# Tails of attentions 3 and 4: batch 2's sum, root and shift moved up, two of four weight loads ahead of the first row fetches, and bias and next preparation placed among the ranks

## The reference

```
x = x + L2_xattn(layernorm(x), ctx)     # attention 3 (l = 2 in the code)
x = x + L2_ffn(layernorm(x))            # its expert stage
x = x + L3_xattn(layernorm(x), ctx)     # attention 4 (l = 3)
x = x + L3_ffn(layernorm(x))            # its expert stage, the last of the kernel
```

```
logits = x @ W_router (+ b_router)              # 8 experts
top_vals, top_idx = top_k(logits, 2)
w = softmax(top_vals)
y_e = act(x @ W1[e] + b1[e]) @ W2[e] + b2[e]    # gelu, 256 hidden, no bias | relu, 512 hidden, biases
out = sum over the two chosen e of w_e * y_e
```

## Time and profile before

| | |
|---|---|
| runs, median of three | 1247.73 us (1243.54 to 1250.17) |
| profiled execution, first to last instruction (span) | 1241.1 us |
| PE busy | 1028.2 us (83%) |
| DVE busy | 756.0 us (61%) |
| POOL busy | 670.2 us (54%) |
| ACT busy | 658.9 us (53%) |
| chain that ended last | PE 53%, DVE 18%, issue 8%, POOL 8%, ACT 7%, DMA 5% |
| mean granted TensorE clock | 0.892 of 2.4 GHz |

### The profile page before, as it was taken

How to read it: one execution, slowest core, us unless ns; L and a number is a source line. 1 busy time by engine, 2 the same in 40 slices (tenths; PEclk the granted TensorE clock), 3 DMA queues, 4 the chain that set the end, 5 groups by cost and what they waited for, 6 DMA issues and landing times.

```text
span 1241.1 us, 22522 instructions
## 1 busy us (share of the span) xinstructions
PE 1028.2 (83%) x6547; PEld 793.3 (64%) x6547; DVE 756.0 (61%) x2570; ACT 658.9 (53%) x2366; POOL 670.2 (54%) x1163
## 2 busy tenths in 40 slices
PE   3984999847899977986999998397699999966993
PEld 3874788734555547774677765386467776645993
DVE  4367254587878776247676687532776676754443
ACT  2225233337888952446887875243387888831321
POOL 5122456546666745257655565647475555655452
PEclk9775899977999995998999999599789999975998
DMA  3422446684920021420000000166300000014566
GB/s 60 4 27 89 131 155 208 202 145 164 389 84 2 2 69 35 136 78 1 19 1 18 18 2 18 41 178 186 96 18 2 1 1 2 2 35 124 172 203 196
DMA packets 132377, 102.82 MB, mean 83 GB/s; under 512 B 34651, under 2 KB 113939, under 8 KB 132256
## 3 DMA queue, kind: packets, MB, share of 16 engines
q1 hardware_dynamic: 121360, 82.38, 24.1%
q0 software_dynamic: 8448, 17.20, 4.2%
q10 hardware_dynamic: 2448, 1.80, 0.6%
HBM read 64.98 MB, written 36.36 MB: 82 GB/s over the span
## 4 chain that ended last, share of the span: by engine, by line
PE 53%; DVE 18%; issue 8%; POOL 8%; ACT 7%; DMA 5%; SPq 1%; DVEq 0%; ACTq 0%; POOLq 0%
PE ps L2645 5%; PE ps L2826 4%; PE ps L2647 4%; PE ps L2646 4%; PE ps L2840 4%; PE ps L2705 3%; ACT ex L1377 3%; DMA xr<-xr_d,src_i 2%; PE ps L2720 2%; POOL yq_d L884 2%; PE ps L2854 2%; POOL pp L1050 2%; PE ps L3318 2%; PE ps L3137 2%; ACT ex L1263 2%
## 5 line engine op out<-in xcount | busy, mean ns | idle before, releaser
L1050 POOL TENSOR_TENSOR pp<-ex,rc 128x256 f32<-128x256 f32 x384 | 236.1, 615 | 202.9 <-DVE rc L2178 144.9
L1263 ACT ACTIVATE ex<-ps,nmx 128x154 f32<-128x154 f32 x512 | 193.9, 391 | 70.5 <-DVE nmx L2173 69.2
L2173 DVE TENSOR_REDUCE nmx<-ps 128x2 f32<-128x308 f32 x256 | 119.4, 469 | 62.3 <-PE ps L2647 61.9
L884 POOL DMA_INDIRECT yq_d<-yq,ids_q x78 | 74.7, 957 | 75.4 <-DVE yq L1908 56.4
L2826 PEld LDWEIGHTS ps<-ident,pp 128*128 128x128 f32 x640 | 74.0, 142 | 57.5 <-POOL pp L1051 49.9
L1377 ACT ACTIVATE ex<-ps,nmx 128x154 f32<-128x154 f32 x256 | 97.4, 393 | 22.9 <-DVE nmx L2038 22.5
L2645 PE MATMUL ps<-kp,q_s 128*128 128x308 f32 x256 | 96.5, 377 | 15.1 <-ACT ex L1263 8.1
L1051 POOL TENSOR_TENSOR pp<-ex,rc 128x52 f32<-128x52 f32 x384 | 105.9, 276 | 0.0
L1263 ACT ACTIVATION_READ_ACCUMULATOR ex<-ps,nmx 128x1 f32 x512 | 105.0, 205 | 0.0
L2826 PE MATMUL ps<-ident,pp 128*128 128x128 f32 x640 | 100.5, 281 | 4.7 <-POOL pp L1051 4.7
L854 POOL TENSOR_TENSOR ln_r<-ln_v,mhalf 128x4 f32<-128x4 f32 x32 | 34.5, 1079 | 88.3 <-DVE ln_v L1659 76.8
(11 more groups left out here) (441 smaller groups left out, 2806.4 us busy)
## 6 DMA issues: line engine op xcount, KB each, us to landing
w_r<-in_L_ffn_W SPq DMA_DIRECT2D x69, 256.0 KB, 3.5
xq_d<-blankq SPq DMA_DIRECT2D x4, 4160.0 KB, 24.5
w_q<-in_L_ffn_W SPq DMA_DIRECT2D x46, 256.0 KB, 3.4
w_q<-in_L_ffn_w SPq DMA_DIRECT2D x46, 128.0 KB, 2.7
xq<-xq_d SPq DMA_DIRECT2D x22, 130.0 KB, 2.2
w_s<-in_L_ffn_W SPq DMA_DIRECT2D x8, 256.0 KB, 7.0
w_e<-in_L_ffn_W SPq DMA_DIRECT2D x8, 256.0 KB, 4.9
acc<-yq_d SPq DMA_DIRECT2D x8, 256.0 KB, 4.5
```

Source lines behind the costliest of these rows:

```text
L884: pool.indirect_dma_start(yq_d[:, :], bass.IndirectOffsetOnAxis(ap=ids_q[:, c:c + 1], axis=0), yq[k % NY][:, h, :], None).then_inc(q_out[k ...
L1050: pool.tensor_tensor(pp[st % 2][:, m % 4, 2 * j:2 * j + 2, :], w[:, :, 0:P], r.broadcast_to([P, 2, P]), ALU.mult)
L1263: ins = act.activation(ex[:, tt % NEX, j, :], ps[:, tt % 3, j * SK:(j + 1) * SK], ACT.Exp, bias=nmx8[:, tt % 8, j:j + 1], accum_out=sm8[:, ...
L2173: dve.tensor_reduce(nmx8[:, tt % 8, :], ps[:, tt % 3, 0:2 * SK].rearrange("p (h s) -> p h s", h=2), AX.X, ALU.max, negate=True).then_inc(n ...
```

## The change

Four things change; all compute what they did.

1. Batch 2. On PE its `tail_sum` stands ahead of batch 1's logits, and its `tail_xT` ahead of the last projection. On DVE the sum stands ahead of batch 1's `best`, its statistics and `tail_shift` ahead of the last two `add_up`. On POOL its root follows the second scatter of batch 0 instead of the eighth, and batch 3's root the third of batch 1 instead of the second. On ACT its `scale` stands ahead of batch 1's `second_rows`. `best(2)` on DVE and `logits(2)` on PE stand ahead of batch 3's sum.
2. SP loads the weights of two runs, not of four, before it waits for the scatters. Those of runs 2 and 3 come after two row fetches each.
3. Attention 3: `prep(3, 0, 0)` and `prep(3, 0, 1)` are placed among the ranks of the tail. They are named `("next", 0, i)` in attention 3's ring, and the helper `prep_of` gives ring and name.
4. Attention 4: `comb` is formed batch by batch (`shared_out`), and the turn of batches 0 and 1 and the bias of batch 0 are placed among the ranks. Banks: turns in 0 and 1, bias in 5 and 6, by turns.

```diff
-    ENDING = [("pt", NST - 1, 1), ("rk", 0), ("pt", NST - 1, 4), ("pt", NST - 1, 3), ("lg", 1), ("y", NST - 2), ("pt", NST - 1, 2), ("f", 2), ("rk", 1), ("y", NST - 1), ("f", 3), ("t", 2),
-              ("lg", 2), ("rk", 2), ("t", 3), ("lg", 3), ("rk", 3)]
+    NEXT = [("next", 0, i) for i in range(PREPS)]
+    ENDING = [None, None] + [[("pt", NST - 1, 1), ("rk", 0), ("pt", NST - 1, 4), ("pt", NST - 1, 3), ("f", 2), ("lg", 1), ("y", NST - 2), ("pt", NST - 1, 2), ("rk", 1), ("t", 2), ("y", NST - 1), ("lg", 2), ("f", 3)]
+                             + NEXT[0:1] * (l == 2) + [("rk", 2), ("t", 3), ("lg", 3)] + NEXT[1:2] * (l == 2) + [("rk", 3)] + NEXT[2:] * (l == 2) for l in (2, 3)]
...
+    def prep_of(l, g, i):
+
+        return (2, ("next", 0, i)) if (l, g) == (3, 0) else (l, ("prep", g, i))
...
                 sp.wait_ge(q_tab, l - 1)
-                for k in range(NQ):
-                    weights(k)
+                weights(0)
+                weights(1)
                 sp.wait_ge(q_xs, 16 * 2 * NT * (l - 1))
-                for k in range(NQ + 2):
-                    rows(k)
+                rows(0)
+                rows(1)
+                weights(2)
+                rows(2)
+                rows(3)
+                weights(3)
+                rows(4)
+                rows(5)
...
                 for i in range(2 * TB):
                     scatter_rows(l, 0, i)
-                rstd(2 * l + 1, 2)
-                for i in range(2):
+                    if i == 1:
+                        rstd(2 * l + 1, 2)
+                for i in range(2 * TB):
                     scatter_rows(l, 1, i)
-                rstd(2 * l + 1, 3)
-                for i in range(2, 2 * TB):
-                    scatter_rows(l, 1, i)
+                    if i == 2:
+                        rstd(2 * l + 1, 3)
...
+                scale(l, 2)
                 second_rows(l, 1)
-                scale(l, 2)
                 tail_xT(l, 2)
                 second_rows(l, 2)
                 shares(l, 2)
+                if l == 2:
+                    prep(3, 0, 0)
+                else:
+                    turned(0)
                 scale(l, 3)
                 tail_xT(l, 3)
                 second_rows(l, 3)
+                if l == 3:
+                    turned(1)
                 shares(l, 3)
                 if l == 2:
-                    for i in range(PREPS):
+                    for i in range(1, PREPS):
                         prep(3, 0, i)
+                else:
+                    turned(2)
+                    turned(3)
...
+            def shared_out(b):
+
+                rows = tiles(b)
+                dve.wait_ge(q_slot, B + b + 1)
+                for c, into in enumerate((comb, comb2)):
+                    ins = dve.tensor_tensor(into[:, rows, :], oh[:, c, rows, :], (xe0, xe1)[c][:, rows, D:D + 1].broadcast_to([P, TB, E]), ALU.mult)
+                link(ins)
+                dve.tensor_tensor(comb[:, rows, :], comb[:, rows, :], comb2[:, rows, :], ALU.add).then_inc(q_comb, 1)
...
                 copy_pt(NST - 1, 3)
+                tail_sum(l, 2)
                 best(l, 1)
-                add_up(NST - 2)
-                tail_sum(l, 2)
                 tail_statistics(l, 2)
                 indices(l, 1)
                 marks(l, 1)
+                tail_shift(l, 2)
+                add_up(NST - 2)
                 low_out(NST - 1, 0)
                 low_out(NST - 1, 1)
                 ranks(l, 1)
                 add_up(NST - 1)
+                best(l, 2)
                 tail_sum(l, 3)
                 tail_statistics(l, 3)
-                tail_shift(l, 2)
-                choose(l, 2)
+                indices(l, 2)
+                marks(l, 2)
                 tail_shift(l, 3)
+                if l == 2:
+                    prep(3, 0, 0)
+                else:
+                    shared_out(0)
                 ranks(l, 2)
+                if l == 3:
+                    shared_out(1)
                 choose(l, 3)
+                if l == 2:
+                    prep(3, 0, 1)
+                else:
+                    add_bias(0)
                 ranks(l, 3)
                 experts_of_runs(l)
                 rows_of_runs(l)
                 if l == 2:
-                    preps(3, 0)
+                    for i in range(2, PREPS):
+                        prep(3, 0, i)
+                else:
+                    shared_out(2)
+                    shared_out(3)
+                    add_bias(1)
+                    add_bias(2)
+                    add_bias(3)
                 region(l)
```

124 lines of the change are left out of this document (65 added, 59 removed).

## The result

| | before | after |
|---|---|---|
| runs beside each other on one chip | 1247.63 us median of 10 (1241.41 to 1251.99) | 1234.12 us median of 10 (1228.54 to 1240.14) |
| span of the profiled execution | 1241.1 us | 1234.2 us |
| ratio, 95% interval | | 0.9912, 0.9892 to 0.9932 |

The ratio says 11.0 us of 1247.63, between 8.5 and 13.5; the two medians are 13.5 apart. The forecast was 10.6 us, and 1237.1 us for the time. The two spans differ by 6.9 us only. Why they differ is half of what this case teaches: each profile is one draw, and that of before was a quick one (last part of the experiments).

A forecast was written before the change was run, and what follows sets the result against it. Table and preparation (attention 3) and bias products (attention 4) held PE, nearly level with fetches behind POOL's late scatters. Gains of 6.1 and 4.5 sum to 10.6 us, taking 1247.73 to 1237.1 us; range 1230.5 to 1243.5.

The forecast's parts named there:

- The mechanism: Both tails: the gain comes through the row scatters, with batch 2 scaled 6.7 us behind POOL's first scatter instead of 15.1.
- my signs: Attention 3: POOL never idle over 1 us between scatters; PE at 1.00 within 5 us of the first turn.
- signs of being wrong: New POOL wait in attention 3, w_q releasing PE last, or something other than the fetch ending PE's idle time.
- Attention 3: Attention 3 and its expert stage: first rows turned 7.8 us sooner, less 1.7 for the clock, gives 6.1 us.
- the variance of batch 3: Attention 3, on DVE: put at 779.3, about the time it had before.
- Landing and fetch: Attention 3: the last scatter lands in 2.4 us and the row fetch leaves 0.5 later, at 809.2.
- The clock: Head of attention 3's expert stage: PE idles before it, the lower clock costs up to 4.2 us, 1.7 taken.
- Attention 4 up to the last scatter: Attention 4: batch 3's logits 1.7 us sooner decide; last scatter at 1133.6, 2.9 sooner, between 2.0 and 3.8.
- Landing: Attention 4's last scatter: lands in 2.3 to 5.5 us, 3.9 taken; first rows turned 4.5 us sooner.
- SP's order: Weight loads on SP: the later weights of runs 2 and 3 cost nothing, in attention 3 at most 1 us.
- Landing unchanged: Rival: attention 4's last scatter still takes 5.5 us to land; gain 9.0 us, time 1238.7; chance 0.12.
- Slower: Rival: PE stays at 1.2 GHz in attention 3's expert stage and becomes the bound; 1271 us; chance 0.04.

The follow-up runs named there:

- root_old: Kernel after, but POOL takes batch 2's root behind all eight scatters of the first batch; 1243.73 us, ratio 0.9982.
- after_again: Kernel after, unaltered, measured again in a later group beside before; 1230.41 us, ratio 0.9901.
- order_fix: Kernel after, but attention 4's ACT scales batch 3 before turning batch 0's shares, PE's turns and first bias product behind the last logits; 1282.56 us, ratio 0.9945.
- root_later: Kernel after, but batch 3's root one scatter later on POOL; 1281.11 us, ratio 0.9934.
- fill4: Kernel after, plus 24 unused identity products on PE ahead of attention 4's first bias product; 1279.73 us, ratio 0.9918.
- fill3b: Kernel after, plus 14 unused identity products on PE between attention 3's last rank and its expert stage; 1228.88 us, ratio 0.9874.
- no_sp: Kernel after, but with SP's old order: weights of four runs, then six row fetches; 1234.45 us, ratio 0.9876.
- sp_fix: Kernel after, with order_fix's edit and SP's old order together; 1230.55 us, ratio 0.9881.

## Why the prediction was right, point by point

**The mechanism.** All steps were there. ACT scales batch 2 6.6 us behind POOL's first scatter (6.7 forecast, had 15.1); ACT stands still for turn(0); POOL waits for batch 3's slots in attention 4; table, preparation and bias products are off the chain. root_old shows that nothing of it comes without the early root. Two of my signs failed: in attention 3 POOL idles 1.27 us among its scatters in the profile, where I had allowed 1 (nothing in after_again), and PE was at 1.00 only 6.3 us behind the first turn, not 5 (4.1 in after_again). On the second chip two signs of being wrong did come, a new wait of POOL in attention 3, and a preparation that ends PE's idle time ahead of the turn; there order_fix, root_later and fill4 have ratios of 0.992 to 0.9945.

**Attention 3.** Last scatter +41.8 forecast: +42.89 in the profile, +41.75 in after_again. The mistake was the variance of batch 3. I put it at 779.3; POOL's root, which starts when it is there, is at 780.60 and waited 1.27. PE carries batch 2's turn and logits ahead of the sum, and part of it fell under the lower clock, which I had counted for attention 4 alone. Landing and fetch, 2.9 forecast, took 2.73. Turned 7.15 sooner (7.8 forecast), 8.24 in after_again. The clock: 1.7 taken from a range of 0 to 4.2; 2.7 and 1.5 measured, of which fill3b shows that the 1.5 are the clock. Net at the first results 6.1 forecast, 4.4 and 6.7 measured, 6.6 to 7.4 with like draws.

**Attention 4 up to the last scatter.** Turned to before's start, the variance was at 1102.09 + 4.00 = 1106.1, at the low-clock end of my range, and from it to the end of the logits are 12.9 us, 12.3 forecast. So batch 3's slots came 0.4 sooner and not 1.7. The last scatter still came 1.7 sooner in the profile and 3.6 in after_again, 2.9 forecast. It came sooner than the slots did because before, POOL was still sending batch 2 when batch 3's slots were there (1127.29 against 1126.01), which I had in the sum.

**Landing.** This term was mis-sized: 3.9 taken as the middle, 4.71 measured. From last scatter to fetch it is 5.16 and 5.27 us with the new order of SP (after, after_again) and 5.35 with the old (no_sp), since the last scatter now starts when two runs' weights are out either way; sp_fix, with all four out, has 5.74. Turn 4.5 sooner forecast, 2.8 and 4.6 measured, 2.3 to 3.1 with like draws.

**SP's order.** I cost the later weights at nothing, and PE waits for no `w_q` in the first four runs. That the order as a whole is worth 0.2 us in the new tail I did not expect: I had given it 1.6 in attention 4.

**The time.** 10.6 us forecast, 11.0 (8.5 to 13.5) measured by the ratio, but the pair of traces on which the steps stand gives 6.9. With like draws it is 6.6 to 7.4 in attention 3, where I had 6.1, and 2.8 to 3.8 in attention 4, where I had 4.5: the mechanism is right, and that the sum is so close is in part luck, since one half was too small and the other too large. I also read 6.6 us as lying around the span. It is 1.7 to 1.9 in every run (after's profiled execution took 1235.95 at a span of 1234.2); the other 5 us were the quick draw of before's profile, and could have told me of it. Against its own executions' median, the forecast of 1237.1 is 3.0 above 1234.12.

**The rivals.** "Landing unchanged" (9.0) was as near as the forecast in its one term: 4.71 lies midway between 3.9 and 5.5. "Slower" did not come: PE was at 1.00 again 6.3 us after the first turn in attention 3 and 4.8 in attention 4.
